# A deformable-convolution kernel: interpolation weights in two buffers by a table of places, and high parts of combined rows on another engine

## The chip, the cores and the metric

One Trainium2 chip, one of its cores. The number that counts is the device time of one execution in microseconds, the median of three runs.

## The reference, cut to what matters

The input x is 4 images of 128 channels and 32 x 32 pixels. Two residual blocks follow each other, each on a group-normalised input (groups of 4 channels):

```python
x = x + _L0_conv_ref(_gn(x), W, b)                  # pixel by pixel mixing
x = x + _L1_conv_ref(_gn(x), w1, b1, w2, b2, wd)    # deformable convolution

# block 1: xn = xf / max(norm over channels, eps)
s  = relu(einsum('bcp,bcq->bpq', xn, xn)) ** 2      # 1024 x 1024 an image
gx = einsum('oc,bcp->bop', W, xf) + b
y  = einsum('bpq,bcq->bcp', s, gx)

# block 2: two 3x3 convolutions make 72 offsets a pixel (4 groups x 9 taps x 2),
# each tap is read at its offset place by bilinear interpolation,
# and the nine sampled images are multiplied by wd, then relu
offset = conv2d_same(conv2d_same(x, w1, b1), w2, b2)
out = relu(deform_conv(x, offset, wd, k=3, pad=1, dg=4))
```

## The kernel before

**Software pipeline.** The four images go through one after the other, but two at a time: while image b is sampled and convolved with `wd` ("back"), image b + 1 is mixed and its offsets are made (`front`), and image b + 2 has its norms prepared (`prepare`). Image 0's front runs alone at the start; the last image's back runs alone at the end. Each engine has its own list of work, written out by hand: a loop over 72 slots n = 9 t + k (tile t of 8, step k of 9), the same on every engine. Constants give the slots: SCORE, MIX and BETWEEN every third slot up to 25; STATS 26, MEAN 32, VAR 35, NORM 36 for the second group norm; COMBINE 37 and 48, CONV 42 and 53 for the two 3x3 convolutions; WRAP_OFF 59, PREP 59 to 65, TURN_OFF 66 and 67, EXTREMES 68. Engines run in order, so a wait holds all that stands behind it on the same engine; semaphores tie the lists together.

**Sampling.** A tile is 4 image rows. For each, VectorE makes `tent` (L1226, L1232, L1235, 128x576 each) out of the positions `pos`, and from it the interpolation weights `wpix` in five products (`weights`, L1251; four of two taps each and one of one tap). TensorE transposes them through two PSUM banks (`turn_weights`, L628, "taps 0" to "taps 4"), ScalarE copies them to `wcell` (L833). "windows 0" are pieces of the image that are turned the same way (L618, L826). `sample` multiplies weights by windows (L650), ScalarE takes the result to `val` (L846). `dconv` (L672) is the convolution with wd, in four parts m of nine taps; part 0 stands in slots 60 to 62, parts 1 to 3 behind the last slot. `wpix` is one buffer, so the weights of tile t + 1, group i, wait until group i of tile t has been transposed; they stand in the slots of tile t:

```python
if t < ROWT - 1 and TURN_SLOT.get(k, "").startswith("taps"):
    weights(b, t + 1, int(TURN_SLOT[k].split()[1]))
```

Tile 0 of the next image is made behind slot 71.

**The 3x3 convolutions.** Four combinations of image rows (v = 0 to 3) halve the products of a 3x3 kernel in one direction. VectorE makes a combination (`combine_rows`, L1049). The product is made in three passes of a high and a low part in fp32r: ScalarE copies the high part (L808), VectorE subtracts it for the low part (`split_rows`, L1053), TensorE multiplies (L485, 18 matmuls for two of the combinations). `middle_sums` (L1062) and `output_rows` (L1075) put the results together. `conv1_done` and `off_done` mark them.

**Norms and scores.** `prepare` normalises image b + 2 (L973), ScalarE squares it (L779), TensorE sums the squares ("norms", L518) and multiplies by W (L523), VectorE floors and inverts the norms (L999, L1002), builds a diagonal of them (`inv2_diag`, L1004, in the buffer `rel`), and TensorE spreads it over all partitions with ones ("spread", L530), ScalarE keeps it in `inv2_all` ("keep", L783). "bias" is L1009 and L1013. `score` makes a block of s (L485 into psB), ScalarE its ReLU (L796), GpSimd its square (L400), `mix` multiplies by gx (L554). L1158 to L1165 add the result and take the statistics, `channel_stats` L953, `group_mean` L510, `spread` L959 to L962, `std` L773, `normalise_x1` L978 and L984.

## Time and profile before

| | us |
|---|---|
| median of 3 runs | 527.44 (527.24 to 530.28) |
| the profiled execution | 531.88 |
| its span | 530.2 |
| TensorE busy | 436.9, 82% |
| VectorE busy | 345.2, 65% |
| ScalarE busy | 225.7, 43% |
| GpSimd busy | 134.1, 25% |
| mean granted TensorE clock | 0.92 |

PE is TensorE's matmul, PEld its weight load, DVE VectorE, ACT ScalarE, POOL GpSimd, SP SyncE. L12 is line 12 of the kernel before. "[3.74 <-DVE varp L962]" behind a row says how long the engine stood idle before it and which instruction released it. The granted clock is a share of full speed, 1.00 being 2.4 GHz and 0.5 being 1.2 GHz; a value between is a mean over the window.

### The profile page before, as it was taken

The page shows a single profiled execution, that of the slowest core. Times are in us where ns is not written, and L with a number is a line of the kernel's source. Part 1 is how long each engine was busy: PE and PEld are TensorE (multiplying, and loading weights), DVE is VectorE, ACT ScalarE, POOL GpSimd, SP SyncE. Part 2 cuts the span into 40 slices and gives each one's busy share as a digit, 9 for nine tenths or more (in the row PEclk, how much of TensorE's full clock was granted, in tenths as well). Part 3 has the DMA queues.
Part 4 walks back from the last instruction along what each step waited for, and adds up shares of the span by engine and source line. Part 5 has one row for each costly group of instructions (what it writes and reads, how often), then busy time and mean ns, then how long its engine had stood idle before and what let it go on. Part 6 is the DMA issues. An engine that isn't in the chain of part 4 may idle for free.

```text
span 530.2 us, 10665 instructions
## 1 busy us (share of the span) xinstructions
PE 436.9 (82%) x3881; PEld 313.4 (59%) x3881; DVE 345.2 (65%) x582; ACT 225.7 (43%) x404; POOL 134.1 (25%) x179
## 2 busy tenths in 40 slices
PE   2896677499959898899967898899967898878876
PEld 2663546266536576676645566676645566656655
DVE  4738964797596855577497765677497766399600
ACT  2242221165534543255544444255544544178540
POOL 3273300087310020056510011056610011031100
PEclk9999687799977897999977899999987899999989
DMA  3400002000100022010000013010000003022111
GB/s 129 153 1 1 0 0 46 0 22 21 28 14 21 22 41 56 11 42 21 21 21 21 21 22 75 11 41 20 21 22 21 21 21 76 31 51 53 41 32 32
DMA packets 22188, 17.27 MB, mean 33 GB/s; under 512 B 1980, under 2 KB 20668, under 8 KB 22140
## 3 DMA queue, kind: packets, MB, share of 16 engines
q1 hardware_dynamic: 21884, 16.07, 11.5%
q10 hardware_dynamic: 256, 0.52, 0.6%
q8 instruction: 35, 0.57, 0.5%
q14 instruction: 13, 0.11, 0.1%
HBM read 3.74 MB, written 3.28 MB: 13 GB/s over the span
## 4 chain that ended last, share of the span: by engine, by line
PE 66%; DVE 18%; ACT 8%; issue 6%; DMA 1%; DVEq 0%; ACTq 0%; SPq 0%
PE psB L485 15%; PE psB L672 12%; PE psA L554 9%; PE psA L485 9%; PE psT L628 7%; PE psV L650 5%; DVE wpix L1251 3%; PE psA L523 2%; PE psB L518 2%; ACT val L846 2%; PE psT L618 2%; ACT wcell L833 2%; DVE tent L1232 1%; DVE combo L1049 1%; DVE tent L1226 1%
## 5 line engine op out<-in xcount | busy, mean ns | idle before, releaser
L1251 DVE TENSOR_TENSOR wpix<-tent 128x512 f32<-128x512 f32 (+1 forms) x160 | 110.0, 726 | 51.0 <-PE psT L628 48.7
L833 ACT ACTIVATE wcell<-psT 128x512 f32<-128x512 f32 (+1 forms) x160 | 84.1, 551 | 103.6 <-PE psT L628 102.6
L628 PE MATMUL psT<-ident,wpix 128*128 128x128 f32 x576 | 91.4, 293 | 19.0 <-ACT wcell L833 7.8
L400 POOL TENSOR_TENSOR sim<-rel 128x512 f32<-128x512 f32 x64 | 78.2, 1242 | 86.0 <-ACT rel L796 85.9
L628 PEld LDWEIGHTS psT<-ident,wpix 128*128 128x128 f32 x576 | 71.1, 150 | 46.6 <-issue 27.0
L425 POOL COPY strips<-hring 128x256 f32<-128x256 f32 x64 | 37.0, 606 | 140.8 <-PE psT L618 140.7
L672 PE MATMUL psB<-val,wd_sb 128*128 128x256 f32 x288 | 68.1, 393 | 3.6 <-ACT val L846 1.8
L672 PEld LDWEIGHTS psB<-val,wd_sb 128*128 128x128 f32 x288 | 55.1, 195 | 14.3 <-issue 6.7
L485 PE MATMUL psA<-combo_p,w_p 128*128 128x512 f32 (+1 forms) x144 | 49.8, 507 | 13.7 <-DVE combo_p L1053 13.7
L554 PE MATMUL psA<-sim,scratch 128*128 128x512 f32 x128 | 60.5, 596 | 0.0
L485 PE MATMUL psB<-g_p 128*128 128x512 f32 x192 | 55.5, 425 | 0.2 <-ACT rel L796 0.2
L650 PE MATMUL psV<-wcell,hwin 64*32 64x144 f32 x2048 | 49.0, 303 | 4.6 <-ACT val L846 2.9
L846 ACT ACTIVATE val<-psV 128x576 f32<-128x576 f32 x64 | 43.8, 685 | 15.6 <-PE psV L650 15.2
L485 PEld LDWEIGHTS psA<-combo_p,w_p 128*128 128x128 f32 (+1 forms) x144 | 30.5, 219 | 28.2 <-DVE combo_p L1053 11.5
L796 ACT ACTIVATE rel<-psB 128x512 f32<-128x512 f32 x64 | 38.1, 598 | 16.3 <-PE psB L485 11.6
L1258 DVE TENSOR_TENSOR yout<-orelu,x_all 128x256 f32<-128x256 f32 x16 | 6.8, 424 | 58.4 <-ACT orelu L851 58.4
L485 PEld LDWEIGHTS psB<-g_p 128*128 128x128 f32 x192 | 35.0, 193 | 10.5 <-issue 3.8
L650 PEld LDWEIGHTS psV<-wcell,hwin 64*32 64x32 f32 x2048 | 29.0, 111 | 17.9 <-issue 17.6
L485 PE MATMUL psB<-combo_p,w_p 128*128 128x512 f32 (+1 forms) x144 | 39.1, 415 | 0.0
L808 ACT ACTIVATE combo_p<-combo 128x544 fp32r<-128x544 f32 x32 | 20.9, 657 | 31.9 <-DVE combo L1049 31.2
L554 PEld LDWEIGHTS psA<-sim,scratch 128*128 128x128 f32 x128 | 23.3, 189 | 18.4 <-issue 15.0
L485 PEld LDWEIGHTS psB<-combo_p,w_p 128*128 128x128 f32 (+1 forms) x144 | 22.9, 166 | 10.2 <-issue 1.3
(143 smaller groups left out, 431.5 us busy)
## 6 DMA issues: line engine op xcount, KB each, us to landing
hwin<-hwin SPq DMA_DIRECT2D x64, 128.0 KB, 2.4
out<-yout SPq DMA_DIRECT2D x16, 128.0 KB, 1.8
x_all<-x SPq DMA_DIRECT2D x1, 1536.0 KB, 10.0
off_scr<-sim SPq DMA_DIRECT2D x4, 288.0 KB
combo<-sim SPq DMA_DIRECT2D x20, 32.0 KB
val<-w SPq DMA_DIRECT2D x1, 576.0 KB
wd_sb<-wd SPq DMA_DIRECT2D x1, 576.0 KB
x_all<-x SPq DMA_DIRECT2D x1, 512.0 KB, 3.5
```

The costliest lines, as they stand in the source:

```text
L400: pool.tensor_tensor(sim[:, i % 2, j * HALF:(j + 1) * HALF], rel[:, j, :], rel[:, j, :], ALU.mult)\
L425: pool.tensor_copy(strips[:, :, odd, :].rearrange("p m (r c) -> p m r c", c=SUP), src)\
L485: last = pe.matmul(dst, left[l], right[r], start=start and i == 0, stop=stop and i == 2)
L554: last = pe.matmul(psA[:, j, :], gxT[:, i, :], sim[:, i % 2, j * HALF:(j + 1) * HALF], start=i == 0, stop=i == QT - 1)
L628: last = pe.transpose(bank[:, at:at + P], wpix[:, k, 2 * h:2 * h + 2, :].rearrange("p g q -> p (g q)"), ident[:, :])
L650: last = pe.matmul(bank[g * CG:(g + 1) * CG, e, :, m, :], hwin[rows, t % 2, u // 2, (u + r) % 2, g * CG:(g + 1) * CG], w[:, :, :, BLK * u: ...
L672: last = pe.matmul(bank, wd_sb[:, k * C:(k + 1) * C], val[:, k, at:at + 2 * P], start=k == 0, stop=k == K - 1)
L796: act.activation(rel[:, j, :], psB[:, j, :], ACT.Relu).then_inc(s["rel_done"], 1)
L808: act.activation(combo_p[:, 0, v], combo[:, v % 2], ACT.Copy).then_inc(s["combo_hi"], 1)
L833: act.activation(wcell[:, t % 2, taps[0]:taps[-1] + 1, :, :].rearrange("q k h p -> q (k h p)"), bank[:, 0:len(taps) * G // 2 * P], ACT.Cop ...
L846: act.activation(dst, src, ACT.Copy).then_inc(s["val_free"], 1)
L1251: dve.tensor_tensor(w, ty, tx, ALU.mult).then_inc(s["weights_done"], 1)
```

## The change

`wpix` gets a second buffer, taken by the tile's parity, so that a group of weights waits for the transposes of the tile two before it. A table W_AT says in which slots the five groups of tiles 2 to 7 are made. Tile 0 of the next image moves to slot 64, tile 1 behind slot 71. The high part of the combined rows becomes a copy on VectorE, just ahead of the subtraction. The slots of the group norm, the convolutions and the preparation move ahead by one to three, and the spread of the norms moves from slot 64 of one image to slot 1 of the next, its diagonal to slot 67 and into the buffer `combo`.

```diff
-        inv2_diag = gsq.rearrange("p (i q) -> p i q", q=P)
+        inv2_diag = combo[:, :, :, :].rearrange("p e i c -> p (e i c)")[:, 0:NPIX].rearrange("p (i q) -> p i q", q=P)
...
-        wpix = sb("wpix", [P, K, G, CELLS])
+        wpix = sb("wpix", [P, 2, K, G, CELLS])
...
-        STATS, MEAN, VAR, NORM = 26, 32, 35, 36
-
-        COMBINE, CONV = (37, 48), (42, 53)
-        WRAP_OFF = 59
-        PREP = {59: "normalise", 60: "square", 61: "norms", 62: "invert", 63: "bias", 64: "spread", 65: "keep"}
-        TURN_OFF = {66: (0, 1), 67: (2, 3)}
-        EXTREMES = 68
+        STATS, MEAN, VAR, NORM = 26, 31, 33, 34
+
+        COMBINE, CONV = (35, 46), (40, 51)
+        WRAP_OFF = 57
+        PREP = {57: "normalise", 58: "square", 59: "norms", 60: "invert", 61: "bias", 67: "diagonal"}
+        SPREAD, KEEP = 1, 2
+        W_AT = {2: (0, 1, 3, 5, 6), 3: (9, 10, 12, 14, 15), 4: (18, 19, 21, 23, 24),
+                5: (39, 39, 40, 41, 42), 6: (43, 43, 52, 53, 53), 7: (54, 54, 55, 55, 55)}
+        TURN_OFF = {63: (0, 1), 64: (2, 3)}
+        FIRST_WEIGHTS, EXTREMES = 64, 66
...
# TensorE
+            def spread_norm2(b):
+
+                pe.wait_ge(s["diag_done"], b + 1)
+                if not isinstance(b, int) or b > 0:
+                    pe.wait_ge(s["pos_done"], 4 * b)
+                for j in range(2):
+                    last = pe.matmul(psA[:, j, :], ones[:, :],
+                                     inv2_diag[:, QT // 2 * j:QT // 2 * (j + 1), :].rearrange("p i q -> p (i q)"),
+                                     start=True, stop=True)
+                last.then_inc(s["spread2_done"], 1)
 
             def score(b, i):
                 if i == 0:
                     pe.wait_ge(s["g_lo_done"], b + 1)
+                    pe.wait_ge(s["floor_done"], b + 1)
...
             def turn_offsets(b, j, prep):
                 if prep is not None:
-                    pe.wait_ge(s["inv2_all_done"], prep + 1)
+                    pe.wait_ge(s["gx_sum_done"], prep + 1)
...
+                if n == SPREAD:
+                    spread_norm2(b)
...
# ScalarE
+                if n == KEEP:
                     act.wait_ge(s["spread2_done"], b + 1)
                     act.activation(inv2_all[:, :], psA[:, :, :].rearrange("p j n -> p (j n)"), ACT.Copy)\
                         .then_inc(s["inv2_all_done"], 1)
...
-                    if 0 <= n - COMBINE[which] < V:
-                        v = n - COMBINE[which]
-                        act.wait_ge(s["combo_done"], V * m + v + 1)
-                        act.activation(combo_p[:, 0, v], combo[:, v % 2], ACT.Copy).then_inc(s["combo_hi"], 1)
...
# VectorE
+                if what == "diagonal":
                     dve.wait_ge(s["inv2_done"], b + 1)
+                    if not isinstance(b, int) or b > 0:
+                        dve.wait_ge(s["extremes_done"], 2 * b)
...
             def split_rows(b, which, v):
+                dve.wait_ge(s["combo_done"], V * (2 * b + which) + v + 1)
+                dve.tensor_copy(combo_p[:, 0, v], combo[:, v % 2]).then_inc(s["combo_hi"], 1)
                 dve.wait_ge(s["combo_hi"], V * (2 * b + which) + v + 1)
...
-                if not (isinstance(b, int) and ROWT * b + t == 0):
-
-                    dve.wait_ge(s["turned"], TGROUPS * (ROWT * b + t - 1) + TURNS.index(f"taps {i}") + 1 + TURNED0)
+                if not (isinstance(b, int) and ROWT * b + t < 2):
+
+                    dve.wait_ge(s["turned"], TGROUPS * (ROWT * b + t - 2) + TURNS.index(f"taps {i}") + 1 + TURNED0)
...
-                        if t < ROWT - 1 and TURN_SLOT.get(k, "").startswith("taps"):
-                            weights(b, t + 1, int(TURN_SLOT[k].split()[1]))
...
+                        for tile, slots in W_AT.items():
+                            for i in range(len(TAPS)):
+                                if slots[i] == n:
+                                    weights(b, tile, i)
+                        if nxt is not None and n == FIRST_WEIGHTS:
+                            for i in range(len(TAPS)):
+                                weights(nxt, 0, i)
                 if nxt is not None:
                     for i in range(len(TAPS)):
-                        weights(nxt, 0, i)
+                        weights(nxt, 1, i)
```

## Rows read from the trace of the kernel before

**Rows 1.** The page: busy time by engine, and ScalarE's copies of combined rows.
```profile
PE 436.9 (82%) x3881; PEld 313.4 (59%) x3881; DVE 345.2 (65%) x582; ACT 225.7 (43%) x404; POOL 134.1 (25%) x179
...
L808 ACT ACTIVATE combo_p<-combo 128x544 fp32r<-128x544 f32 x32 | 20.9, 657 | 31.9 <-DVE combo L1049 31.2
```

**Rows 2.** Windows: busy us of each engine, granted clock (PEclk), DMA share, GB/s.
```profile
270.00:275.00 5.00, 1.29 (x6) 1.29 (x7) 4.72 (x12) 0.95 (x2) 0.00 (x0) 0.57 0.00 0
284.50:297.00 12.50, 12.50 (x89) 9.66 (x82) 5.99 (x10) 4.22 (x8) 0.75 (x2) 0.87 0.00 1
297.00:301.30 4.30, 2.10 (x43) 1.40 (x42) 3.94 (x7) 2.07 (x4) 0.00 (x0) 1.00 0.28 63
318.60:322.40 3.80, 3.74 (x33) 3.74 (x34) 2.73 (x4) 1.52 (x3) 0.78 (x3) 1.00 0.48 92
82.90:86.20 3.30, 0.00 (x0) 0.00 (x0) 2.17 (x5) 1.06 (x2) 0.87 (x2) 1.00 0.00 0
86.20:93.30 7.10, 7.05 (x32) 6.77 (x32) 2.82 (x4) 0.94 (x1) 0.00 (x0) 0.52 0.38 85
```

**Rows 3.** Timeline, 268 to 279 us: start, duration, operation, [idle before <-releaser].
```profile
268.38 0.21 DVE L953 BATCH_NORM_AGGREGATE mv<-bn 128x2 f32<-128x12 f32 x1 [0.15 <-DVE bn L1165]
...
268.65 0.38 PE L510 MATMUL psB<-mv,avg 128*128 128x1 f32 x2 [1.04 <-DVE mv L953]
...
270.77 2.50 DVE L1251 TENSOR_TENSOR wpix<-tent 128x512 f32<-128x512 f32 x4
273.18 0.15 DVE L959 COPY mean<-psB 128x1 f32<-128x1 f32 x1
...
273.71 0.59 PE L510 MATMUL psB<-varp,avg 128*128 128x1 f32 x2 [3.74 <-DVE varp L962]
...
274.33 0.26 ACT L773 ACTIVATE sd<-psB,eps_col 128x1 f32<-128x1 f32 x1 [3.57 <-PE psB L510]
...
278.64 1.55 DVE L1049 TENSOR_TENSOR combo<-hpad 128x544 f32<-128x544 f32 x2
```

**Rows 4.** Timeline: one tile's weights, from 334.40 us.
```profile
334.40 0.74 DVE L1226 TENSOR_TENSOR tent<-pos,cells 128x576 f32<-128x576 f32 x1
...
336.57 2.83 DVE L1251 TENSOR_TENSOR wpix<-tent 128x512 f32<-128x512 f32 x5
```

**Rows 5.** Groups by line and shape on VectorE, 262 to 348 us.
```profile
L1053 DVE TENSOR_TENSOR combo_p<-combo,combo_p 128x544 fp32r<-128x544 f32 x8 | 5.8, 722 | 0.3
...
L1049 DVE TENSOR_TENSOR combo<-hpad 128x544 f32<-128x544 f32 x4 | 3.0, 767 | 0.0
...
L1194 DVE TENSOR_REDUCE extremes<-combo 72x1024 f32 x2 | 2.3, 1204 | 0.0
...
L1004 DVE TENSOR_TENSOR rel<-ident,inv 128x1024 f32<-128x1024 f32 x1 | 1.2, 1224 | 0.0
```

**Rows 6.** Line 1235 over the whole span: ns min/median/max.
```profile
L1235 DVE TENSOR_SCALAR tent<-tent x32: 459/460/1182, 102.8 to 495.7; 128x576 f32<-128x576 f32 x32
```

**Rows 7.** Timeline: second convolution and norms, b = 1, and output taps of b = 0.
```profile
199.97 2.70 PE L672 MATMUL psB<-val,wd_sb 128*128 128x256 f32 x6
...
301.30 2.73 PE L485 MATMUL psA<-combo_p,w_p 128*72 128x512 f32 x6 [1.95 <-DVE combo_p L1053]
...
311.19 3.17 PE L485 MATMUL psB<-combo_p,w_p 128*72 128x512 f32 x12
...
314.49 0.69 DVE L1075 TENSOR_TENSOR sim<-rel,psA 72x512 f32<-72x512 f32 x1 [0.94 <-PE psB L485]
...
318.66 1.95 PE L518 MATMUL psB<-ones,rel 128*128 128x1 f32 x16 [0.21 <-ACT rel L779]
```

**Rows 8.** Timeline and chain: the first transposes and the first mixing matmul, b = 0.
```profile
104.09 1.11 PE L628 MATMUL psT<-ident,wpix 128*128 128x128 f32 x4 [3.63 <-DVE wpix L1251]
...
110.64 1.72 PE psA L554 x4
```

**Rows 9.** Waits of TensorE, 462 to 498 us: us in total, times, longest.
```profile
PE psT L628 <- DVE wpix L1251: 0.5, 1, 0.5
```

More of the change, by code:

```diff
@@ L525, in prepare @@
                     last.then_inc(s["gx_done"], 1)
-                if what == "spread":
-                    pe.wait_ge(s["diag_done"], b + 1)
-                    pe.wait_ge(s["gx_sum_done"], b + 1)
-                    for j in range(2):
-                        last = pe.matmul(psA[:, j, :], ones[:, :],
-                                         inv2_diag[:, QT // 2 * j:QT // 2 * (j + 1), :].rearrange("p i q -> p (i q)"),
-                                         start=True, stop=True)
-                    last.then_inc(s["spread2_done"], 1)
+            def spread_norm2(b):
[7 more added lines that the diff above has]
+                last.then_inc(s["spread2_done"], 1)
             def score(b, i):
@@ L549, in mix @@
                     pe.wait_ge(s["inv2_all_done"], b + 1)
-                    if not isinstance(b, int) or b > 0:
-                        pe.wait_ge(s["pos_done"], 4 * b)
                 for j in range(2):
@@ L653, in sample, with dconv @@
                 last.then_inc(s["sampled"], 1)
-            def dconv(b, m, nxt, taps):
+            def dconv(b, m, nxt, prep, taps):
                 q = QORDER[m]
@@ L663, in dconv @@
                         pe.wait_ge(s["off_done"], 2 * nxt + 2)
+                    if m == 1 and prep is not None:
+                        pe.wait_ge(s["floor_done"], prep + 1)
                     if m >= 2:
@@ L729, in batch_steps @@
                             first = 3 * DCONV0_AT.index(n)
-                            dconv(b, 0, nxt, range(first, first + 3))
+                            dconv(b, 0, nxt, prep, range(first, first + 3))
                         if nxt is not None:
@@ L733, in batch_steps @@
                 sample(b, ROWT - 1, 0)
-                dconv(b, 1, nxt, range(K))
+                dconv(b, 1, nxt, prep, range(K))
                 sample(b, ROWT - 1, 1)
                 for m in range(2, 4):
-                    dconv(b, m, nxt, range(K))
+                    dconv(b, m, nxt, prep, range(K))
             pe.nop().then_inc(s["turned"], TURNED0)
@@ L780, in prepare, with front @@
                     act.activation(g_p[:, 0], g_sb[:, :], ACT.Copy).then_inc(s["g_hi_done"], 1)
-                if what == "keep":
+            def front(b, n, prep):
+                if prep is not None and n in PREP:
+                    prepare(prep, PREP[n])
+                if n == KEEP:
                     act.wait_ge(s["spread2_done"], b + 1)
@@ L784, in prepare @@
                         .then_inc(s["inv2_all_done"], 1)
-            def front(b, n, prep):
-                if prep is not None and n in PREP:
-                    prepare(prep, PREP[n])
                 if n in SCORE:
@@ L1012, in prepare @@
                     dve.wait_ge(s["gx_sum_done"], b + 1)
+                    dve.wait_ge(s["inv2_done"], b + 1)
                     dve.tensor_tensor(gxT, gxT, inv2[:, :].unsqueeze(2).to_broadcast([P, QT, C]), ALU.mult)\
@@ L1396, in _ @@
                         split_weights(i)
-                if n == EXTREMES - 1:
+                if n == FIRST_WEIGHTS:
                     for i in range(len(TAPS)):
@@ L1401, in _ @@
                     cell_table()
+            for i in range(len(TAPS)):
+                weights(0, 1, i)
             dve.tensor_scalar(tap_at[:, :, 1:2], tap_at[:, :, 1:2], block_col[:, :], None, ALU.add)\
```

6 lines of the change are left out of this document (3 added, 3 removed).

## The prediction

> **What bounds the kernel now.** I read the page first [rows 1]: TensorE is busy 436.9 of 530.2 us, VectorE 345.2, ScalarE 225.7. So most of the time is TensorE's own work, and an edit that moves none of it can only win where TensorE stands still or runs at half clock. The windows of the second batch (b = 1) show where that is [rows 2]: in 270.0 to 275.0 TensorE is busy 1.29 us at a granted clock of 0.57, and in 297.0 to 301.3 it is busy 2.10 of 4.30 us. In the first of these the timeline [rows 3] shows who is late. The channel statistics of the mixed image are ready at 268.59. The small matmul on them runs at once, but VectorE, which is in order, has the tents and four products of tile 4 (the products 2.50 us, from 270.77) ahead of the three small operations that continue the chain, so these start at 273.18; TensorE's second small matmul waits 3.74 us for them. ScalarE's root ends at 274.59, and the reciprocal that needs it again stands behind weights: the first combined row begins at 278.64, and the first convolution fills TensorE from 284.5 on [rows 2], 15.9 us after the statistics. ScalarE adds to it: its 32 copies of combined rows take 657 ns each and it waited 31.9 us in front of them [rows 1], in order, with the evacuations of psT behind it.
>
> The price of one tile's weights on VectorE is 5.0 us (334.40 to 339.40 [rows 4]: 2.17 us of tents, then 2.83 us of products).
>
> **Part by part, batch b = 1 as the model.**
>
> Statistics to first convolution. With the table of places tiles 2, 3 and 4 are made during the mixing, where TensorE is the bound and VectorE waits for it, and nothing lies between slot 24 and slot 39. VectorE then does the three small operations right after the first small matmul, done by about 269.6. TensorE's second one stands behind two groups of transposes and a sample in its own order, about 2.0 us of work after 268.65: 270.8. From that matmul's start to the root's end took 0.88 us in [rows 3] (273.71 to 274.59), and reciprocal, normalisation and release some 1.1: the first combined row starts near 272.75, where it was 278.64. A combination and a subtraction take 0.77 and 0.72 us [rows 5]. The added copy on VectorE is not in the trace; its nearest row is the single-source operation on 128x576 at 460 ns (1182 at most) [rows 6]. I take 0.45 us; the range is 0.4 to 1.18. So the first low part is ready 1.45 + 0.45 + 0.75 = 2.65 us later, at 275.4, and all four rows take 7.5 us with the copies (eight operations at 0.71 and four at 0.45). TensorE needs until about 276 to reach the convolution, which is now 2 slots earlier in its order (1.65 us of transposes and a sample are behind it instead of ahead). The convolution starts at 276 and not 284.5: 6.9 us won.
>
> By the Trainium skill, "VectorE: DVE Perf Modes", section "The perf-mode tier table", an fp32 copy from SBUF to SBUF runs at two elements a cycle where a two-input operation gets one. By the fixed term and the clock on that page the copy is an estimate of 0.44 us; the trace agrees for the single-source row.
>
> First to second convolution. VectorE is now the late one, and I walk its list: rows 272.75 to 280.25; tile 5 to 285.25; tents and two products of tile 6 (2.17 + 1.3) to 288.7; the two middle sums, of the size of an output row (0.69 us [rows 7], a pair 1.28 as they overlap a little), to 290.0; the two output rows to 291.3 (TensorE's matmuls for them end near 288.5, 276 and the 12.5 of before, so they wait for VectorE); then 2.65 to the first low part: 293.95. Before, this convolution began at 301.30 [rows 7]: 7.35 us won at the same place in TensorE's order.
>
> Second convolution to the next image's norms. VectorE: rows to 298.8, rest of tile 6 (1.8) to 300.6, tents and two products of tile 7 to 304.05, middle sums to 305.3, rest of tile 7 to 307.1, output rows from there. Before, norms followed the output rows by 4.17 us (314.49 to 318.66 [rows 7]), of which 0.6 was a product that is gone: norms start at 310.7. TensorE ends its convolution at 293.95 + 13.06 - 0.6 = 306.4, and here the change costs something: norms move from slot 61 to 59, ahead of all the output convolution, and only two groups of transposes (1 us) are left as cover. TensorE stands still some 3.3 us. Against 318.66 it is 7.96 us earlier, with 3.7 us of work (a last pair of transposes, a sample, six taps) still to do: 4.25 us of the 7.35 are left. Then the clock. Norms and products ran in 3.7 us at full clock in [rows 2] (318.6 to 322.4), but in 7.05 us at 0.52 where they followed 3.3 us of standing still (82.9 to 86.2, then 86.2 to 93.3). I take the second: 3.4 us lost, 0.85 left. The offsets' transposes no longer stand behind the copy of the spread norms, which I put at 1.2 us won (nothing to 2): 2.0 for this batch. The spread itself (four matmuls of 128x512, some 1.7 us at full clock and 1.95 otherwise) only moves into the next batch's slot 1, where its diagonal is long ready. ScalarE's copy follows it there, and two groups and a score hide it; without that cover it would cost about 1 us a batch, the length of a ScalarE pass over 1024 elements.
>
> The Trainium skill ("TensorE: Matmul & The Clock Gate", "Loop structure matters more than you think") says that long waits between bursts of matmuls send them to half rate. The trace agrees with 0.52 in that window.
>
> The other batches. b = 0 has the same distances to its norms, but runs its output taps after them at half clock (six in 2.70 us [rows 7]) and lost some 3 us there that the new order does not lose again: 5.0 won. b = 2 has no next image to prepare, so nothing is given back: 7.35 won.
>
> The last batch has only weights to make. Between 462 and 498 us TensorE's matmuls waited once, 0.5 us, for VectorE [rows 9], so the second buffer is worth 0.5, at most 2 us if VectorE's start on tile 1 also held it.
>
> The first image. Its diagonal now comes behind the bias at the start (TensorE scores first, then stands 2 us for it, where before it waited for the bias and spread first): 0.5 lost. Copies on VectorE add 0.45 us ahead of each convolution. At its end the spread is taken out and the first transposes of batch 0, at 104.09 [rows 8], come at about 102.7 even with that. But then the diagonal stands behind the rest of tile 0's weights (2.1), the extremes (2 x 1.2) and its own 1.22 us [rows 5]: 108.3. TensorE has a score and two groups until 106.6 and waits. The spread, windows, a group and a score put the first mixing matmul at 113.6 instead of 110.64 [rows 8]. Loss with the 0.5: 3.5 us.
>
> The rest, at nothing: the wait for the floored norms ahead of the scores (they end 3 us earlier), the diagonal in the combined rows' buffer (its readers are done by slot 66), tile 1 of the next batch at VectorE's end. That last adds 5 us to a list with an output add behind it; by my walk the add is 4 to 5 us ahead of the ReLU that waits for it.
>
> **Sum.** 531.88 - 5.0 - 2.0 - 7.35 - 0.5 + 3.5 = 520.5 us for a profiled execution. The profiled one of before is 4.44 us above the median of its runs (527.44), which I take off: 516.0.
>
> **Rivals.**
> A. Norms at full clock. The standing still is 3.3 us by my walk, and a microsecond less may not let the clock fall (the window 297.0 to 301.3 stands half idle and has 1.00 [rows 2]). 3.4 us more in two batches: 509.2.
> B. Given back at half clock. The first matmuls of each convolution are slow after a wait, the window 284.5 to 297.0 shows 0.87. If the output taps behind the norms, the convolutions and the mixing's start each lose more, 2.5 us in three batches, the time is 523.5. For it: VectorE as the bound leaves TensorE waiting in short pieces; against it: TensorE's idle time shrinks in total.
> C. VectorE's copy is slow: slower than before. The single-source operation of 460 ns took 1182 where GpSimd worked beside it [rows 6]. At 1.18 us a copy, the 8 of each of three batches and 2 of the first image, all on the chain, cost 26 x 0.73 = 19.0 us: 531.88 - 11.35 + 19.0 = 539.5, less 4.4 is 535.1. It decides from 0.45 + 11.35/26 = 0.89 us. Against it: GpSimd is busy 0.00 us in 297.0 to 301.3 and 0.75 in 284.5 to 297.0 [rows 2]. The Trainium skill ("GPSIMD Engine Reference", "Specifications") has VectorE and GpSimd share SBUF interfaces when VectorE uses both of its ports, the rule that speaks against the change; the trace agrees, by 460 against 1182 ns.
> D. The change does not do what it says: the chain of statistics starts no sooner because the weights of tile 4 still wait, now for transposes of tile 2, and stand in front of it. Then only the last batch wins and the first image loses: 527 to 530.
>
> **Chances.** Forecast 0.46, A 0.20, B 0.18, C 0.08, D 0.08. The range goes from somewhat under A to between B and D: 507 to 526; the unknown copy at 0.7 us (26 x 0.25 = 6.5) is inside. One per cent, about what a measurement can tell from no change, is 522.2 to 532.7. The forecast and A are below it but for a few hundredths, and a third of B: faster 0.70, same 0.20, slower 0.10.
>
> **What would show it.** In the changed profile: the combined rows' first operation about 4.2 us after the statistics (was 10.1); copies near 0.45 us on VectorE, no such copies on ScalarE; TensorE waiting about 3 us for ScalarE's square ahead of the norms in b = 0 and 1, with norms and products in 7 us; the next output rows gated by VectorE, not by TensorE; a wait for the diagonal at the start of batch 0 alone. Wrong if copies take over 0.9 us, if tents or products of tile 4 lie behind the statistics, or if TensorE is so much slower in the convolutions that VectorE's walk is not what binds.

## The result, and the profile after

| | before | changed | ratio (95%) |
|---|---|---|---|
| median us, 20 executions each | 529.91 | 526.37 | 0.9944 [0.9919, 0.9968] |
| profiled execution / its span | 531.88 / 530.2 | 530.77 / 528.7 | |

The change wins 0.6%, which is inside what counts here as no difference. The forecast was 516.0 us with a range of 507 to 526; the changed kernel lies just above the range. An execution more than 1.5% above the fastest of its kernel counts as disturbed and is left out of every ratio, but not out of the medians. The profiled execution of the changed kernel is the longest of its 20, 4.4 us above their median, and that of the kernel before is 2.0 above its own; so the traces show less of the win than the medians do. The busy line of the page and the group of VectorE's copies:

```profile
PE 435.3 (82%) x3881; PEld 311.0 (59%) x3881; DVE 356.7 (67%) x614; ACT 206.9 (39%) x372; POOL 136.0 (26%) x179
```

```profile
L1060 DVE CAST combo_p<-combo x32: 435/436/642, 61.1 to 419.3; 128x544 fp32r<-128x544 f32 x32
```

Against [rows 1] the 32 copies have gone from ScalarE (18.8 us less) to VectorE (11.5 more), at 436 ns each where 450 were forecast. TensorE's own work is the same, and its mean granted clock is 0.92 as before.

Where the time went is read best by stages, cut at the end of the last mixing matmul in each batch (TensorE's rows `psA<-sim,scratch` in the timeline). The first column is image 0's front and the mixing of image 1; "batch 0" and "batch 1" run from the end of mixing in that batch to the end of mixing in the next one; "batch 2" runs to the end of its output convolution, and "last batch" from there to the end of the last one (4 to 5 us of the span lie behind it). The kernels of the lower rows are explained with their experiments.

| stage, us | start to end of mixing in batch 0 | batch 0 | batch 1 | batch 2 | last batch |
|---|---|---|---|---|---|
| before | 141.5 | 122.7 | 119.8 | 77.4 | 64.1 |
| changed | 150.2 | 119.5 | 117.1 | 76.0 | 61.9 |
| forecast difference | +3.5 | -5.0 | -2.0 | -7.35 | -0.5 |
| measured difference | +8.7 | -3.2 | -2.7 | -1.4 | -2.3 |
| e6, copies alone | 143.1 | 120.7 | 115.7 | 71.5 | 61.9 |
| e12, spread, norms and turns as before | 145.1 | 114.3 | 112.7 | 70.8 | 61.9 |
| e1, diagonal first | 143.7 | 118.3 | 117.1 | 76.1 | 62.1 |
| e2, offsets turned later | 149.2 | 117.2 | 117.8 | 69.9 | 62.4 |
| e3, norms later | 146.9 | 115.0 | 113.0 | 74.8 | 64.4 |
| e4, copies back on ScalarE | 145.8 | 119.6 | 119.2 | 73.4 | 61.9 |
| e5, copies made twice | 146.1 | 120.1 | 119.5 | 72.5 | 62.2 |
| e7, all three | 144.1 | 112.3 | 112.2 | 71.2 | 62.4 |
| e10, all three, copies on ScalarE | 141.3 | 111.5 | 112.2 | 73.8 | 63.9 |

Some of it is scatter: before its first mixing matmul e2, e3 and the changed kernel run the same code, and it begins at 27.44, 25.38 and 28.66; the last batch reads 61.9 to 64.4 without an edit to it. A difference under 2 us in one cell is not a finding, and in the first column and in batch 2 one under 3.5 is not.

**Statistics to convolution, b = 1.** The timeline of the changed kernel where [rows 3] were:

```profile
273.86 0.21 DVE L956 BATCH_NORM_AGGREGATE mv<-bn 128x2 f32<-128x12 f32 x1 [0.15 <-DVE bn L1174]
...
274.62 0.16 DVE L962 COPY mean<-psB 128x1 f32<-128x1 f32 x1 [0.55 <-PE psB L513]
...
275.82 0.38 PE L513 MATMUL psB<-varp,avg 128*128 128x1 f32 x2
...
277.77 1.36 DVE L1056 TENSOR_TENSOR combo<-hpad 128x544 f32<-128x544 f32 x2
...
279.05 0.64 DVE L1060 CAST combo_p<-combo 128x544 fp32r<-128x544 f32 x1
279.72 0.79 DVE L1062 TENSOR_TENSOR combo_p<-combo,combo_p 128x544 fp32r<-128x544 f32 x1
...
280.57 1.73 PE L488 MATMUL psA<-combo_p,w_p 128*128 128x512 f32 x6 [1.07 <-DVE combo_p L1062]
```

Nothing stands ahead of VectorE's three small operations now, and the wait of 3.74 us for `varp` is gone. The first combined row begins 3.70 us after the statistics (274.07 to 277.77; it was 10.05), and the convolution 10.95 us after the end of mixing (269.62); before, it began 20.36 after it. The second convolution starts 29.56 after it against 37.15, so 7.6 us earlier.

**Norms.** TensorE stands idle in front of them, as forecast, because ScalarE's square is late:

```profile
312.57 1.04 PE L634 MATMUL psT<-ident,wpix 128*128 128x128 f32 x8
316.70 1.95 PE L521 MATMUL psB<-ones,rel 128*128 128x1 f32 x16 [3.10 <-ACT rel L787]
318.51 3.66 PE L526 MATMUL psA<-w_sb,inv_all 128*128 128x128 f32 x16
```

```profile
312.73:316.70 3.97, 0.88 (x8) 0.64 (x6) 2.41 (x5) 1.70 (x3) 2.23 (x5) 1.00 0.33 67
316.70:322.20 5.50, 5.50 (x34) 5.45 (x34) 1.51 (x3) 1.38 (x2) 0.72 (x3) 0.69 0.44 101
...
446.60:453.30 6.70, 6.70 (x33) 5.24 (x34) 6.12 (x10) 0.71 (x2) 0.00 (x0) 0.62 0.00 0
```

The same two groups took 3.7 us at clock 1.00 in [rows 2]; here, behind 3.10 us of standing still, they take 5.5 at 0.69.

**End of batch 2.** This was not forecast. The last line above belongs to `dconv` part 1, and the timeline shows what precedes it:

```profile
441.03 2.19 SPq L315 DMA_DIRECT2D hwin<-hwin  x2
...
445.46 1.22 PE L656 MATMUL psV<-wcell,hwin 64*32 64x144 f32 x32 [2.19 <-DMA hwin<-hwin]
...
446.61 6.63 PE L680 MATMUL psB<-val,wd_sb 128*128 128x256 f32 x18
```

In the kernel before, at the same place:

```profile
442.04 1.37 SPq L312 DMA_DIRECT2D hwin<-hwin  x2
```

```profile
442.16 0.29 PE L582 MATMUL psA<-ident,combo 72*128 72x72 f32 x2
...
445.24 0.72 PE L650 MATMUL psV<-wcell,hwin 64*32 64x144 f32 x32
447.00 0.72 PE L650 MATMUL psV<-wcell,hwin 64*32 64x144 f32 x32 [1.05 <-ACT val L846]
447.66 4.15 PE L672 MATMUL psB<-val,wd_sb 128*128 128x256 f32 x18
```

SP moves the last tile's windows from one place of `hwin` to another, in two transfers, and `sample` needs both. Before, the offsets' transposes at slots 66 and 67 were TensorE's work in that time; its sample starts 5.0 us after the first issue (442.04 to 447.00), and waits 1.05 us for ScalarE, not for the transfer. The change moves the transposes to 63 and 64, ahead of the issue. TensorE is ready 2.2 us after the issue, stands 2.19 us for the transfer (441.03 to 445.46 in all), and then runs 18 matmuls in 6.63 us instead of 4.15.

How much this costs differs between kernels with the same slots here. e5 (and e4 alike) shows

```profile
440.54 1.37 SPq L316 DMA_DIRECT2D hwin<-hwin  x2
...
443.83 0.72 PE L657 MATMUL psV<-wcell,hwin 64*32 64x144 f32 x32 [1.05 <-DMA hwin<-hwin]
444.49 4.15 PE L681 MATMUL psB<-val,wd_sb 128*128 128x256 f32 x18
```

Its two transfers landed 2.4 us after their issues; in the changed kernel they took 3.2 and 3.6 us. So the uncovered transfer costs 1.1 us of waiting and 2.5 us of slower matmuls more when it happens to be slow, and the trace of the changed kernel has such a case. Before, a transfer 1 us slower would still have been hidden: there both had landed 1.6 us before the sample started. The table of TensorE's waits of the changed kernel has the transfer as one of its larger rows:

```profile
PE psA L488 <- DVE combo_p L1062: 22.8, 8, 4.9
PE psB L521 <- ACT rel L787: 12.4, 4, 3.4
PE psB L513 <- DVE mv L956: 8.5, 4, 4.4
PE psV L656 <- DMA hwin<-hwin: 6.3, 4, 2.2
...
PE psA L535 <- DVE combo L1010: 5.0, 2, 3.1
```

Before, the wait for `hwin<-hwin` was 1.6 us in one piece, and ScalarE's squares held TensorE for 6.7 us in all.

**First image.** TensorE's waits for the new diagonal, 5.0 us in two, fall in the start and at slot 1 of batch 0:

```profile
19.64 3.93 POOL L403 TENSOR_TENSOR sim<-rel 128x512 f32<-128x512 f32 x2 [13.57 <-ACT rel L803]
20.61 2.06 DVE L1010 TENSOR_TENSOR combo<-ident,inv 128x1024 f32<-128x1024 f32 x1
...
22.73 3.78 PE L535 MATMUL psA<-combo,ones 128*128 128x512 f32 x4 [3.11 <-DVE combo L1010]
```

```profile
109.02 2.33 DVE L1203 TENSOR_REDUCE extremes<-combo 72x1 f32<-72x1024 f32 x2
111.46 1.39 DVE L1010 TENSOR_TENSOR combo<-ident,inv 128x1024 f32<-128x1024 f32 x1
```

The first diagonal takes 2.06 us and not the 1.22 of [rows 5], because GpSimd squares scores beside it: the scores now come first. Behind the wait the spread takes 3.78 us and the next six score matmuls 3.30, both about half speed, and the first mixing matmul is at 28.66 where it was at 24.48. At batch 0 the second wait is 1.92 us, the spread takes 3.06, and mixing starts at 119.08 instead of 110.48.

Of these 8.6 us 4.2 lie ahead of the first mixing matmul and 4.4 between the end of image 0's mixing and the first mixing matmul of batch 0: 67.7 us where it was 63.2. The moved spread is not what makes this stretch long: e12, which has it at its old place, takes 67.4. The copies are the larger part: the changed kernel with the copies on ScalarE (e4) takes 64.6, and e10 takes 64.5 against 67.7 in e7. In e4 the second convolution starts 1.2 us earlier after the mixing; 1.5 us come only at the second wait (1.35 us) and the spread behind it (1.98), both shorter.

### The profile page after: what moved, and what is told of

Same layout as the page of the kernel before. It is cut to its first block, busy times and chain, and to the rows that moved or that the text cites. A ratio compares the mean times of both kernels' runs of the same rounds, so it can differ in the third digit from the quotient of the medians.

```text
span 528.7 us, 10660 instructions
## 1 busy us (share of the span) xinstructions
PE 435.3 (82%) x3881; PEld 311.0 (59%) x3881; DVE 356.7 (67%) x614; ACT 206.9 (39%) x372; POOL 136.0 (26%) x179
## 3 DMA queue, kind: packets, MB, share of 16 engines
HBM read 3.74 MB, written 3.28 MB: 13 GB/s over the span
## 4 chain that ended last, share of the span: by engine, by line
PE 58%; DVE 25%; issue 6%; ACT 5%; DMA 3%; SPq 1%; DVEq 0%; ACTq 0%; POOL 0%
PE psB L680 12%; PE psB L488 11%; PE psA L558 10%; PE psT L634 5%; PE psA L488 5%; PE psV L656 4%; DVE wpix L1260 4%; PE psA L526 3%; DVE combo L1056 2%; DVE combo_p L1062 2%; DMA hwin<-hwin 2%; PE psT L624 2%; PE psA L535 2%; PE psB L521 2%; DVE combo_p L1060 2%
## 5 line engine op out<-in xcount | busy, mean ns | idle before, releaser
L1260 DVE TENSOR_TENSOR wpix<-tent 128x512 f32<-128x512 f32 (+1 forms) x160 | 106.5, 719 | 35.0 <-PE psT L634 32.6
L634 PE MATMUL psT<-ident,wpix 128*128 128x128 f32 x576 | 85.5, 279 | 10.7 <-ACT wcell L836 6.1
L634 PEld LDWEIGHTS psT<-ident,wpix 128*128 128x128 f32 x576 | 66.6, 143 | 36.6 <-issue 23.0
L428 POOL COPY strips<-hring 128x256 f32<-128x256 f32 x64 | 39.0, 637 | 131.1 <-PE psT L624 130.9
L680 PEld LDWEIGHTS psB<-val,wd_sb 128*128 128x128 f32 x288 | 56.3, 199 | 15.1 <-issue 7.0
L488 PE MATMUL psB<-g_p 128*128 128x512 f32 x192 | 57.2, 435 | 0.0
L488 PEld LDWEIGHTS psA<-combo_p,w_p 128*128 128x128 f32 (+1 forms) x144 | 29.0, 211 | 39.5 <-DVE combo_p L1062 18.8
L656 PE MATMUL psV<-wcell,hwin 64*32 64x144 f32 x2048 | 46.9, 292 | 6.3 <-DMA hwin<-hwin 6.3
L656 PEld LDWEIGHTS psV<-wcell,hwin 64*32 64x32 f32 x2048 | 27.8, 107 | 18.1 <-issue 18.1
L829 ACT ACTIVATE hwin<-psT 128x512 f32<-128x512 f32 x32 | 19.1, 598 | 28.7 <-PE psT L624 28.7
```

The source lines that it names most:

```text
L428: pool.tensor_copy(strips[:, :, odd, :].rearrange("p m (r c) -> p m r c", c=SUP), src)\
L488: last = pe.matmul(dst, left[l], right[r], start=start and i == 0, stop=stop and i == 2)
L634: last = pe.transpose(bank[:, at:at + P], wpix[:, t % 2, k, 2 * h:2 * h + 2, :].rearrange("p g q -> p (g q)"), ident[:, :])
L656: last = pe.matmul(bank[g * CG:(g + 1) * CG, e, :, m, :], hwin[rows, t % 2, u // 2, (u + r) % 2, g * CG:(g + 1) * CG], w[:, :, :, BLK * u: ...
L680: last = pe.matmul(bank, wd_sb[:, k * C:(k + 1) * C], val[:, k, at:at + 2 * P], start=k == 0, stop=k == K - 1)
L829: act.activation(hwin[:, t % 2, :, 0, :], bank.rearrange("q (m c) -> q m c", c=C), ACT.Copy)\
```

## The experiments

All were compared with the kernel before, on the same chip; ratios are given with 95% intervals, and spans are those of the profiled execution.

**e1. The diagonal ahead of the bias for image 0.**

```diff
                 pe.wait_ge(s["diag_done"], b + 1)
+                pe.wait_ge(s["gx_sum_done"], b + 1)
...
-            for what in PREP.values():
+            for what in ("normalise", "square", "norms", "invert", "diagonal", "bias"):
                 prepare(0, what)
```

> The changed kernel with one edit: at the start, for image 0 alone, VectorE builds the diagonal of the norms ahead of the bias and not behind it (TensorE's spread then also waits for the bias). In the trace of the changed kernel TensorE stands 3.11 us for this diagonal, and the spread (3.78 us) and the score behind it (3.30 us) then run at about half speed; the first mixing matmul is at 28.66 us, 24.48 in the kernel before. Theory (waiting and then the clock): the diagonal is ready before the bias, the first mixing matmul comes at about 25.5, and 3 to 4 us are won against the changed kernel, ratio to the kernel before about 0.988. Rival (GpSimd's squares, 3.93 us for the first pair, hold the first mixing matmul, whatever TensorE does): first mixing matmul later than 27.5 and under 1 us won.

Ratio 0.9879 [0.9836, 0.9922], 521.25 us, span 521.3. With the diagonal made early TensorE does not wait, and the spread takes half as long:

```profile
17.45 1.64 PE L488 MATMUL psB<-g_p 128*128 128x512 f32 x6
19.10 1.95 PE L536 MATMUL psA<-combo,ones 128*128 128x512 f32 x4
...
22.28 1.90 PE L559 MATMUL psA<-sim,scratch 128*128 128x512 f32 x4
```

The first mixing matmul is at 22.28, 6.4 us earlier than in the changed kernel, and 2.2 earlier than before the change. Part of this is scatter: with this start it stands at 22.3 to 24.1 in four kernels (e1, e7, e10, e11), with the changed kernel's start at 25.4 to 28.7 in five, and with the start of before at 24.0 to 26.3 in four. The stages of batches 1 and 2 are unchanged.

**e2. Offsets' transposes back at slots 66 and 67, weights, extremes and diagonal behind them.**

```diff
-        PREP = {57: "normalise", 58: "square", 59: "norms", 60: "invert", 61: "bias", 67: "diagonal"}
+        PREP = {57: "normalise", 58: "square", 59: "norms", 60: "invert", 61: "bias", 69: "diagonal"}
...
-        TURN_OFF = {63: (0, 1), 64: (2, 3)}
-        FIRST_WEIGHTS, EXTREMES = 64, 66
+        TURN_OFF = {66: (0, 1), 67: (2, 3)}
+        FIRST_WEIGHTS, EXTREMES = 67, 68
```

> The changed kernel with the offsets' transposes back in slots 66 and 67, behind the last tile's windows, tile 0's weights in 67, extremes in 68, diagonal in 69. In the changed kernel's batches 1 and 2 TensorE waits 1.31 and 2.19 us in front of tile 7's first sample for the windows' transfer between partitions, and in batch 2 the nine taps behind it take 6.63 us, 4.15 in the kernel before. Theory (the transfer lost its cover when the offsets' transposes moved ahead of the windows): the wait at that sample is gone or under 0.5 us, the taps take 4.15 us, 1 to 2 us are won in b = 0 and 1 and 4 to 5 in b = 2; 5 to 8 us in all, ratio 0.980 to 0.985. Rival (VectorE's longer list at the batch's end, tiles 0 and 1, extremes, diagonal, is what the end waits for): that list starts 2.4 us later, the output adds become late, and the time is the same as the changed kernel's or longer, ratio 0.994 or more.

Ratio 0.9884 [0.984, 0.9927], 522.6 us, span 520.6. At the end of batch 2:

```profile
439.75 0.73 PE L656 MATMUL psV<-wcell,hwin 64*32 64x144 f32 x32 [1.05 <-ACT val L849]
440.41 4.15 PE L680 MATMUL psB<-val,wd_sb 128*128 128x256 f32 x18
```

The wait for the transfer is gone there and the 18 matmuls take 4.15 us. Batch 2 is 6.1 us shorter, batch 0 by 2.3, batch 1 not at all. Of the 6.1 us 1.0 had come before the edit's slots, in the second convolution, which ran 12.35 us and not 13.37; 2.5 are the 18 matmuls; the rest, 2.7, is the shorter wait and the order. In all five kernels with the offsets' transposes at 66 and 67 behind the same table (e2, e7, e10, e11, e12), the wait at this sample is 1.05 us and for ScalarE, and the 18 matmuls take 4.15 or 4.16; in the five with 63 and 64 (the changed kernel, e1, e3, e4, e5) it is for the transfer, 1.05 to 2.30 us, and they take 4.15 to 6.63. That the cover is what e2 restores is shown; that it is worth 6 us is shown for a slow transfer only. The edit also moves tile 0's weights, extremes and diagonal, and that part was not tried alone.

**e3. Norms two slots later (61, invert 62, bias 63).**

```diff
-        PREP = {57: "normalise", 58: "square", 59: "norms", 60: "invert", 61: "bias", 67: "diagonal"}
+        PREP = {57: "normalise", 58: "square", 61: "norms", 62: "invert", 63: "bias", 67: "diagonal"}
```

> The changed kernel with norms, invert and bias at slots 61, 62 and 63 instead of 59, 60 and 61, so that a group of transposes, a sample and six output taps stand ahead of the norms on TensorE again. In the changed kernel TensorE waits 3.10 us for ScalarE's square in b = 1, and the products with W take 3.66 us, 2.0 in the kernel before. Theory (this wait and the half clock behind it gave back a good part of what the convolutions had won): no wait above 0.5 us at the norms, products in about 2 us, 3 to 5 us won in each of b = 0 and 1, 6 to 10 in all, ratio about 0.980. Rival (TensorE is held later anyway, by the offsets' transfer, by the windows' transfer or by the bias in front of the offsets' transposes): the wait turns up there, under 2 us won, ratio above 0.990.

Ratio 0.9845 [0.9793, 0.9896], 519.5 us, span 518.1. Norms now stand behind a sample and twelve matmuls of the output convolution:

```profile
307.11 2.86 PE L680 MATMUL psB<-val,wd_sb 128*128 128x256 f32 x12
309.81 1.84 PE L521 MATMUL psB<-ones,rel 128*128 128x1 f32 x16
311.51 2.03 PE L526 MATMUL psA<-w_sb,inv_all 128*128 128x128 f32 x16
```

No wait, and 3.73 us for both. Batch 0 is 4.5 us shorter than in the changed kernel, batch 1 4.2: about the wait of 3.10 us and the 1.8 us that norms and products take longer behind it. The forecast had 3.3 and 3.4 us for the two and took them for the price of the change.

**e4. The changed kernel with the copies back on ScalarE.**

```diff
+                        act.wait_ge(s["combo_done"], V * m + v + 1)
+                        act.activation(combo_p[:, 0, v], combo[:, v % 2], ACT.Copy).then_inc(s["combo_hi"], 1)
...
-                dve.tensor_copy(combo_p[:, 0, v], combo[:, v % 2]).then_inc(s["combo_hi"], 1)
```

> The changed kernel with the high parts copied by ScalarE again (the table of places, the two buffers and the slots stay). Theory 1 (VectorE is the bound from the statistics to the norms, 8 copies of 0.43 us lie on its list in each batch): both convolutions' ends and the norms come 2 to 3.4 us earlier in each batch, 5 to 9 us less than the changed kernel, ratio about 0.980. Theory 2 (ScalarE in its order would hold TensorE's transposes as much as the copies hold VectorE, as 2.24 and 1.01 us waits in front of transposes in the kernel before): no gain, ratio 0.992 to 1.0.

Ratio 0.9916 [0.9879, 0.9953], 524.11 us, span 524.4. Beside the rest of the change the move of the copies is worth nothing that can be told: the intervals overlap. In batch 1 the first convolution starts 12.3 us after mixing (10.95 with the copies on VectorE), but the second ends at 41.9 against 43.1. Norms and products then take 7.2 us, about the 7.05 of the forecast, where the changed kernel's take 5.5. The first image is 4.4 us shorter, 3.1 of them behind its mixing.

**e5. Every copy on VectorE made twice.**

```diff
+                dve.wait_ge(s["combo_hi2"], V * (2 * b + which) + v)
+                dve.tensor_copy(twin[:, :, :], combo[:, v % 2]).then_inc(s["combo_hi2"], 1)
```

> The changed kernel with each copy of a combined row on VectorE made twice (the second into a buffer that nothing reads): 32 more copies of 0.43 us. Theory (VectorE's list is the bound from the statistics to the norms): in each batch the second convolution's end and the norms come 3 to 3.4 us later and the time grows by 8 to 11 us, ratio to the kernel before 1.010 to 1.015. Rival (TensorE's own work and ScalarE's evacuations bound that stage, VectorE only here and there): under 1.2 us a batch, 0 to 4 us in all, ratio 0.995 to 1.002.

Ratio 1.0024 [0.9982, 1.0066], 531.18 us. By the medians 4.8 us more for the 32 extra copies, whose own time is 32 x 0.44 = 14 us; the profiled execution is the shortest of its ten (span 524.5) and nothing of it is seen, so the price is not well settled. In batch 1 the second convolution starts 1.3 us later, where the five extra copies ahead of it are 2.2, and ends 0.35 later, where the eight are 3.5. So VectorE's list binds up to the start of the second convolution, with little room, and not up to its end. The norms begin 0.8 us later, and norms and products take 7.1 us and not 5.5, so that batch 1 is 2.4 us longer; batch 2 is 3.5 shorter, with the transfer that is not slow.

**e6. The kernel before, with the copies alone moved.**

```diff
-                        act.activation(combo_p[:, 0, v], combo[:, v % 2], ACT.Copy).then_inc(s["combo_hi"], 1)
...
+                dve.tensor_copy(combo_p[:, 0, v], combo[:, v % 2]).then_inc(s["combo_hi"], 1)
```

> The kernel before with one part of the change: the high parts of the combined rows are copied by VectorE, everything else stays. Theory: two effects of the same size. ScalarE no longer holds the transposes in front of the first convolution (2.24 and 1.01 us of waiting in front of it), which starts 1 to 2 us earlier; the low part that starts the second one comes 0.4 us later and VectorE's weights with it. Ratio 0.995 to 1.003. Rival (the copy costs its length wherever it stands, as VectorE is on the chain there): 3.4 us a batch, ratio 1.01 to 1.02.

Ratio 0.9778 [0.9715, 0.9842], 520.23 us, span 517.0: this part alone wins 2.2%, more than the whole change and outside both expectations. By the medians of all executions it is 1.8% (529.53 to 520.23). What it removes is seen in the kernel before. One row of its timeline, then TensorE's waits in 262 to 300 us:

```profile
280.78 0.97 PE L628 MATMUL psT<-ident,wpix 128*128 128x128 f32 x4 [2.24 <-ACT hwin L826]
```

```profile
PE psT L628 <- ACT hwin L826: 2.2, 1, 2.2
PE psT L628 <- ACT wcell L833: 1.3, 2, 1.0
```

and the same stretch with the copies on VectorE:

```profile
PE psT L628 <- ACT wcell L829: 0.6, 2, 0.3
```

```profile
281.05 4.82 PE L485 MATMUL psA<-combo_p,w_p 128*128 128x512 f32 x18 [0.74 <-DVE combo_p L1051]
```

Before, ScalarE stood 2.85 us in front of the first copy, waiting for a combined row, and `hwin`, for which TensorE was waiting, stood behind that copy. The convolution starts 3.2 us earlier (17.2 after mixing, was 20.36), with the wait for `varp` of 3.7 us still there.

**e13. The kernel before, ScalarE's copies three slots later.**

```diff
-                    if 0 <= n - COMBINE[which] < V:
-                        v = n - COMBINE[which]
+                    if 0 <= n - COMBINE[which] - 3 < V:
+                        v = n - COMBINE[which] - 3
```

> The kernel before with the high parts still copied by ScalarE, but three slots later in its list (slots 40 to 43 and 51 to 54 and not 37 to 40 and 48 to 51), so that the evacuations of three groups of transposes stand ahead of the first copy. The kernel before with the copies on VectorE had a ratio of 0.9778, its first convolution beginning 3.2 us earlier after the mixing and its 18 first matmuls taking 4.82 us and not 6.07. Theory (it was ScalarE's order, not its time: in its list the copies wait for VectorE's rows and hold the evacuations that TensorE's transposes need): about as much is won without any work on VectorE, ratio 0.975 to 0.988. Rival (the copies' 0.66 us and the extra hand-over between two engines were the cost): the later place makes it worse or no better, ratio 0.997 or more.

Median 520.67 us against 529.39 of the kernel before (0.984 by the medians; no ratio with an interval is given, as one of its six executions took 511.79 us and the others 519.65 to 521.31). Every one of the six is shorter than the shortest of the kernel before in that session, 525.65. The profiled one took 520.05. Its first convolution of batch 1 starts 16.9 us after mixing, as early as in e6. Its waits of TensorE in 262 to 300 us lack the one for `hwin`, as in e6, although ScalarE makes every copy at 658 ns:

```profile
PE psT L628 <- ACT wcell L833: 0.6, 2, 0.3
```

```profile
ACT combo_p L808 <- DVE combo L1049: 2.5, 4, 0.9
```

So in the kernel before the place of the copies in ScalarE's order costs nearly all of the time that e6 wins (8.7 of 9.3 us by the medians), and not the copies' own length or the engine that makes them.

**e7. e1, e2 and e3 together on the changed kernel.** The diagonal stands at slot 69.

> The changed kernel with the three edits together: diagonal ahead of the bias for image 0, offsets' transposes behind the last windows (slots 66 and 67), norms, invert and bias at 61 to 63. Alone they gave ratios of 0.9879, 0.9884 and 0.9845, where the changed kernel had 0.9944: 3.4, 3.2 and 5.2 us. Theory (three waits at three places): they add up to 10 to 13 us, ratio 0.970 to 0.976. Rival (the last two are both at a batch's end and fill the same hole, or VectorE's list at the end becomes late when all stands later): no better than 0.980.

Ratio 0.9572 [0.9531, 0.9613], 507.73 us, span 506.3, mean clock 0.942. It beats both kernels. It is 18.6 us under the changed one by the medians; the three edits alone took off 5.1, 3.8 and 6.9, 15.8 in all, so they add up and a little more (by the ratios 11.9 us for the three alone and 19.7 for e7, more than the expectation). Its waits, the largest and those of the norms and the transfer:

```profile
PE psA L488 <- DVE combo_p L1063: 22.0, 8, 4.9
...
PE psB L521 <- ACT rel L788: 6.2, 2, 3.4
...
PE psV L657 <- DMA hwin<-hwin: 1.6, 1, 1.6
```

**e10. e7 with the copies on ScalarE.** The edit is that of e4.

> The kernel with the three edits, and with the high parts copied by ScalarE again. With the copies on ScalarE the changed kernel had 0.9916 against 0.9944. Theory (VectorE's list ends the second convolution's results, 1.2 us a batch came back there in the trace): ratio 0.002 to 0.006 under that of the kernel with three edits. Rival (ScalarE's order costs as much, in front of the first convolution, which began 1.3 us later in that trace): same ratio within 0.002.

Ratio 0.9575 [0.9522, 0.9629], 508.82 us: no difference from e7. That is a balance and not an absence of effects: the first image is 2.8 us shorter, batch 2 is 2.6 longer, and there TensorE again waits twice 1.29 us for ScalarE ahead of the first convolution, which starts 12.7 us after mixing and not 10.6.

**e11. e7 with the spread at slot 3 and the keep behind the ReLUs.**

```diff
-        SPREAD, KEEP = 1, 2
+        SPREAD, KEEP = 3, 3
```

> The changed kernel with the three edits, and the spread of the norms behind the second score (slot 3) with ScalarE's copy behind that score's ReLUs. Theory (in batch 0 the wait for the diagonal, 2 us, and the half clock behind it are covered by a score; in b = 1 and 2 the first mixing matmul then waits about 1 us for the copy): 1 to 3 us won against 0.9572, ratio 0.952 to 0.956. Rival (the copy's wait and GpSimd's squares, now later, cost as much in three batches): 0.957 or more.

Ratio 0.9673 [0.9622, 0.9725], 510.9 us: 1% worse than e7, by the intervals (which do not touch). The profiled stages differ by at most 2.3 us and not all one way, so where the 1% arises stays open.

**e12. The changed kernel with the spread, its diagonal and keep at their old slots 64 and 65, norms at 61, transposes at 66 and 67.** It differs from e6 by the second buffer, the table of places and the earlier slots of group norm, convolutions, wrapped offsets, normalising and the next image's tile 0 alone.

> The kernel before with two buffers, the table of places, the copies on VectorE and the earlier slots, but with spread, diagonal and its copy where they stood before (slots 64, 65, diagonal in the buffer of the ReLUs), norms at 61, offsets' transposes at 66 and 67. Against the changed kernel with three edits (0.9572) it differs only in the place of the spread. Theory 1 (the moved spread costs: the wait for its diagonal at the start of batch 0, then half clock): the first mixing matmul of batch 0 comes 3 to 5 us earlier after the offsets, the other batches lose under 1 us each at their ends, ratio 0.950 to 0.955. Theory 2 (what is lost at the start is won back at the ends of b = 0 and 1, where the offsets' transposes wait for the spread's copy): ratio 0.956 to 0.962.

Ratio 0.9682 [0.9633, 0.9732], 511.84 us, span 508.9. The chain of kernels before, e6, e12, changed splits the change, by profiled spans: copies 530.2 to 517.0, 13.2 us won; buffer, table and earlier slots 517.0 to 508.9, 8.1 won; the moves of spread, norms and offsets' transposes 508.9 to 528.7, 19.8 us lost. By the medians, free of the long profiled execution of the changed kernel, it is 9.3 won, 8.4 won and 14.5 lost. By stages, e12 against e6 wins 6.4, 3.0 and 0.7 us in the three batches and loses 2.0 in the first image. The last part costs about the same in four stages (5.1, 5.2, 4.4 and 5.2 us), most of which e1, e3 and e2 give back.

Neither expectation for e12 came true. It differs from e7 only in the place of the spread and is 4.1 us slower by the medians, and the ratio intervals do not touch. So the move of the spread is right in itself; what cost was the order of diagonal and bias at the start, the early norms and the early offsets' transposes.

## Why the prediction was wrong, point by point

It had the direction, and too large an effect: 11.4 us were forecast and 3.5 measured by the medians. In the absolute time 2.5 us more come from the start value: three executions gave 527.44 for the kernel before, twenty give 529.91. By the stages the forecast sum was -11.35 us and the measured one -0.9; the difference of 10.4 is 5.2 at the first image, 5.95 in batch 2 and 1.8 in batch 0, less 0.7 and 1.8 that batches 1 and last gave more. These are single executions, with the scatter told above.

- **Statistics to first convolution: right.** Start forecast at 276, 11.85 us after the end of mixing; measured 10.95. The copy was 0.44 us against 0.45. The largest rival on the bad side, C, is out: 642 ns was its longest. D is out too, as the chain shortened as drawn.
- **Second convolution: right, with a walk that held to its start.** 7.6 us against 7.35. The first convolution's output rows began 3.7 us after its last matmul (291.56 to 295.24; before 0.13), so VectorE was the late list, as walked. Behind the second convolution the walk failed: the output rows wait for TensorE, and e5 shows room.

```profile
312.87 0.69 DVE L1084 TENSOR_TENSOR sim<-rel,psA 72x512 f32<-72x512 f32 x1 [0.64 <-PE psB L488]
```

- **Norms uncovered: right.** Wait 3.3 forecast, 3.10 measured, and the clock fell, though less far: 5.5 us against 7.05 (7.2 and 7.1 in e4 and e5). Batch 1 came to -2.7 where -2.0 was forecast, and rival A did not happen. In batch 0, -5.0 was a guess by likeness and -3.2 was measured; the spread, moved into the next image's mixing, takes 1.9 us there.
- **"b = 2 has no next image to prepare, so nothing is given back": the step that failed first.** The second convolution kept its gain (28.96 us after mixing, 36.74 before), and it was still there at the offsets' transposes (50.35 against 58.2). It was lost behind them. The forecast asked what the moved transposes wait for, and gave them 1.2 us of gain; it did not ask what they covered. Without them TensorE stands 2.19 us for the windows' transfer, and the 18 matmuls behind it take 6.63 us and not 4.15. e2 gives 6.1 us back, 5.1 of them behind the second convolution.
- **First image, +3.5: right in kind, mis-sized.** The order of waits was as forecast, and the second wait 1.92 us. At the start, 0.5 was forecast and 4.2 measured (0.9 to 4.2 among kernels with the same code there), since the wait was 3.11 and not 2, the diagonal 2.06 and not 1.22, and nothing was put down for the clock after it. The same omission stands at batch 0, where the spread took 3.06 us and not 1.9. e1 takes 6.5 us off the stage. Behind image 0's mixing 3.0 us were forecast and 4.4 measured; the forecast gave 0.9 of this to the copies and the rest to the second wait, but e4 gives back 3.1 us with the copies, and e12 shows the stretch just as long without the moved spread. Rival B named this ("the mixing's start") but priced it at 2.5 a batch in later batches.
- **Last batch.** 0.5 forecast for the second buffer. Up to its first output convolution the batch takes 37.20 us where it took 37.26, so the buffer is worth nothing there; the 2.3 us come from a wait and a clock behind it, which also differ between kernels with the same code.
- **What the sum did not see.** It counted the copies as a cost on VectorE and the table as the source of the gain. In truth [rows 1] already had the hint, ScalarE waiting 31.9 us in front of its copies, and the forecast mentions it and prices nothing. e6 and e13 show 9 us of medians in it. The two gains overlap: with the whole chain short, e10 is no slower in all with the copies on ScalarE.

By the Trainium skill, "TensorE: Matmul & The Clock Gate", section "Loop structure matters more than you think", matmuls behind a long wait run at half rate. The traces agree at the three places where the change made a wait (1.92, 2.19 and 3.10 us); the 3.97 us that held 0.88 us of matmuls ahead of the norms still showed 1.00 themselves, the fall came in the next stretch. In e3 the spread behind 3.16 us did not run slower (1.98 us), so such a wait did not always bring it.

## What to carry to other kernels

Work that is moved ahead of a wait leaves the place where it was: ask of each moved block which transfer or which other engine's operation ran behind it, not only what it waits for. A new wait of 2 to 3 us of TensorE was worth 4 to 5 us here where the matmuls behind it ran at or near half clock. And an in-order engine's wait in front of a cheap operation is to be read with what stands behind it: moving 0.66 us copies by three slots was worth more than the whole change (8.7 and 3.5 us by the medians).

## What the runs showed of the hardware

- A VectorE operation with two SBUF inputs also slows beside GpSimd: the diagonal (128x1024) took 2.06 us in the start, beside GpSimd's two products (3.93 us), and 1.22 in e1, where GpSimd stood idle. The Trainium skill, "GPSIMD Engine Reference", section "Specifications", names two SBUF inputs as a case of contention; the forecast had used only the other case.
- The clock did not fall equally behind equal waits. Behind 3.10 us the norms and products took 5.5 us (0.69 granted), in the kernel before 7.05 behind 3.3 us of standing still (0.52, [rows 2]); in e3 and the changed kernel, behind diagonals of the same 2.06 us and waits of 3.16 and 3.11 us, the spread took 1.98 and 3.78 us. What decides between the two was not tried.
- A transfer inside SBUF on SP's queue (`hwin<-hwin`, 128 KB) landed 2.3 to 2.5 us after its issue in 49 of 64 cases in the changed kernel and in 52 in the kernel before, and took up to 3.6 us in the one and 3.9 in the other, without an edit to it. What has to be covered is the slow case.
